# Expert rows scaled by their gates at eviction, and gathers that add into the result

## The reference, cut to what matters

```python
x = hidden_states                                   # 625 x 1024, after layernorm
capacity = ceil(2 * 1.25 * 625 / 8)                 # 196 slots for each of 8 experts
combine, dispatch = _top2_gating(x @ router_w, capacity)
expert_in = einsum('nec,nh->ech', dispatch, x)
hmid = silu(einsum('ech,ehf->ecf', expert_in, w1) + b1)
expert_out = einsum('ecf,efh->ech', hmid, w2) + b2
y = einsum('nec,ech->nh', combine, expert_out)      # two gates g1, g2 for each node
shared = silu(x @ sw1 + sb1) @ sw2 + sb2
out = y + 0.1 * shared
```

## Time and profile before

| | us |
|---|---|
| median of 3 runs | 1152.14 |
| lowest and highest | 1151.02, 1152.32 |
| the profiled execution, its own time | 1163.16 |
| its span | 1161.4 |
| busy in it: PE, PEld | 1099.8, 920.4 |
| busy in it: DVE, ACT, POOL | 697.3, 385.3, 380.6 |

### The profile page before, as it was taken

The page is one execution under the profiler, slowest core; times in us unless marked ns, Lnnn a source line. Parts: engine busy times, 40 slices in busy tenths (PEclk is TensorE's granted clock), DMA queues, the critical chain, the costliest instruction groups (busy, mean ns, idle before and its releaser), DMA issues.

```text
span 1161.4 us, 14333 instructions
## 1 busy us (share of the span) xinstructions
PE 1099.8 (95%) x5505; PEld 920.4 (79%) x5505; DVE 697.3 (60%) x1376; ACT 385.3 (33%) x599; POOL 380.6 (33%) x262
## 2 busy tenths in 40 slices
PE   5999999999999999994999999899979999999896
PEld 4878888888888888884999999887756878888774
DVE  8476666666655652100777676657378748866546
ACT  3222222222222222213223333362333415336652
POOL 6036556456556466651422132000020000310016
PEclk8999999999999999997999999899989999989997
DMA  8965677777666555539665543362242111588757
GB/s 326 416 199 131 157 198 203 204 205 178 160 159 151 120 119 118 112 49 268 186 205 165 176 120 100 103 208 91 73 76 88 30 62 38 218 260 262 246 179 247
DMA packets 84611, 191.77 MB, mean 165 GB/s; under 512 B 29079, under 2 KB 45274, under 8 KB 76088
## 3 DMA queue, kind: packets, MB, share of 16 engines
q1 hardware_dynamic: 36362, 123.40, 33.6%
q0 software_dynamic: 31968, 35.38, 14.4%
q10 hardware_dynamic: 16206, 32.00, 9.4%
HBM read 136.60 MB, written 54.15 MB: 164 GB/s over the span
## 4 chain that ended last, share of the span: by engine, by line
PE 72%; DMA 9%; DVE 8%; POOL 5%; issue 2%; ACT 2%; POOLq 0%; DVEq 0%; SPq 0%
PE ps L482 61%; POOL adj_scratch L1871 5%; DMA stage<-in_w_e 3%; DMA adj_scratch<-cnt,idx 3%; DVE rl L340 2%; PE ps L724 2%; PE ps L761 2%; PE ps L688 2%; DVE EQ L1248 1%; PE ps L472 1%; DMA stage<-h_scratch 1%; ACT rh L331 1%; PE ps L772 1%; DMA stage<-in_w_rel 1%; DMA AT<-adj_scratch 1%
## 5 line engine op out<-in xcount | busy, mean ns | idle before, releaser
L340 DVE TENSOR_TENSOR rl<-stage,rh 128x512 fp32r<-128x512 f32 (+1 forms) x288 | 228.7, 824 | 334.4 <-ACT rh L331 334.4
L331 ACT CAST rh<-stage 128x512 fp32r<-128x512 f32 (+1 forms) x288 | 193.7, 708 | 528.7 <-PE ps L482 289.7
L1871 POOL DMA_INDIRECT adj_scratch<-cnt,idx x162 | 261.5, 1614 | 224.3 <-DMA adj_scratch<-cnt,idx 81.5
L482 PE MATMUL ps<-rh,xTh 128*125 128x512 f32 x800 | 317.1, 396 | 2.0 <-DVE U L1316 1.7
L482 PE MATMUL ps<-rl,xTh 128*125 128x512 f32 x800 | 315.4, 394 | 0.0
L482 PE MATMUL ps<-rh,xTl 128*125 128x512 f32 x800 | 314.9, 394 | 0.0
L482 PE MATMUL ps<-rh,Ar 125*125 125x342 f32 x600 | 194.5, 329 | 20.6 <-DVE rl L340 10.9
L482 PE MATMUL ps<-rl,Ar 125*125 125x342 f32 x600 | 193.5, 327 | 0.0
L482 PEld LDWEIGHTS ps<-rh,xTh 128*125 128x125 f32 x800 | 148.7, 186 | 39.8 <-DVE U L1316 2.1
L482 PEld LDWEIGHTS ps<-rh,xTl 128*125 128x125 f32 x800 | 149.0, 186 | 37.3
L482 PEld LDWEIGHTS ps<-rl,xTh 128*125 128x125 f32 x800 | 149.0, 186 | 36.3
(11 more groups left out here) (263 smaller groups left out, 1195.5 us busy)
## 6 DMA issues: line engine op xcount, KB each, us to landing
stage<-in_w_rel SPq DMA_DIRECT2D x32, 1024.0 KB, 6.7
stage<-h_scratch SPq DMA_DIRECT2D x24, 855.0 KB, 6.5
stage<-in_w_e SPq DMA_DIRECT2D x16, 1024.0 KB, 6.1
adj_scratch<-Z POOLq DMA_DIRECT2D x16, 767.0 KB, 22.5
KR<-key_scratch ACTq DMA_DIRECT2D x27, 384.0 KB, 3.7
h_scratch<-He ACTq DMA_DIRECT2D x40, 257.0 KB, 10.1
h_scratch<-He ACTq DMA_DIRECT2D x40, 256.0 KB, 9.0
stage<-in_w_gate SPq DMA_DIRECT2D x8, 1024.0 KB, 6.3
```

Of the source, the lines that this page charges most:

```text
L331: e.copy(h, s).then_inc(*a_hi.up(*[("hi", t) for t in step(i)]))
L340: e.tensor_tensor(l, s, h.bitcast(F32), ALU.subtract).then_inc(*v_lo.up(*[("lo", t) for t in step(i)]))
L482: ins = e.matmul(ps[0:P, b, 0:width], a, m, start=first and n == 0, stop=last and n == len(parts) - 1)
L1871: e.indirect_dma_start(accd, bass.IndirectOffsetOnAxis(ap=idx[:, n:n + 1], axis=0), cnt[:, n:n + 1], None, compute_op=ALU.add).then_inc(*d ...
```

## The change

- A new array in memory, `gate_scratch`, one float for each slot, is zeroed by one more small store in the list of zeros. After the slots of expert 1 are asked for, POOL scatters g1 and g2 of every node to it (ten indirect transfers of 125 floats), waits for them, and loads it to `sg` (98 x 16, one column for each pair of expert and half; `sg[p, m]` is float 98 m + p). Slots of expert 2 and later are asked for behind that.
- ScalarE's copy to `EOs` becomes an ACTIVATE with a scale read from `sg`, and waits for `sg`.
- The ten gathers add into X, first all of k = 0, then all of k = 1, each in the order of chunks 3, 4, 0, 1, 2. They wait for X's second biases of their chunk, and the second for the first of the same chunk. The multiplications and additions of `combine`, ScalarE and POOL are gone.
- The second biases of half 1 for chunks 3 and 4 move from behind `routed_out(7)` to ahead of `routed_out(5)`, on TensorE and VectorE.
- `own`, VectorE's last additions and the stores go by halves first, then by chunks in the order 3, 4, 0, 1, 2, no longer by chunks and then halves. VectorE's last additions wait for both gathers of their chunk.

```diff
+    gated = nc.dram_tensor("gate_scratch", (128 * 23, 1), F32, kind="Internal").ap()
+        sg = sb("sg", [HC, 2 * 8], F32)
+        d_go, d_gi = count("gates_out", 16), count("gates_in", 16)
+        zeros.append((gated.rearrange("(p q) o -> p (q o)", p=128), Z[:, 0:23]))
-        gathered = [U128[:, i, :] for i in range(C)] + [G[:, i, :] for i in range(7, 10)] + [BA128[:], BB128[:]]
+        LAST = (3, 4, 0, 1, 2)
@@ sync
-            for c in range(C):
-                for hf in range(2):
+            for hf, c in [(hf, c) for hf in range(2) for c in LAST]:
@@ tensor
+                if n == 5:
+                    second_biases(1, range(3, C))
                 routed_out(n)
             routed_out(6)
             routed_in(7)
             second_biases(1, range(3))
             routed_out(7)
-            second_biases(1, range(3, C))
...
-                for j in range(2):
-                    on.wait_ge(*at("own low", j, hf))
+                on.wait_ge(*at("own low", 1, hf))
...
+            for hf in range(2):
+                for c in LAST:
+                    own(c, hf)
@@ scalar
-                        e.copy(EOs[:, m % 3, HALF[hf]], ps[0:HC, banks.of["out", n, j, hf], :]).then_inc(*a_out.up(("eo", n, j, hf)))
+                        on.wait_ge(*at("gates in"))
+                        e.activation(EOs[:, m % 3, HALF[hf]], ps[0:HC, banks.of["out", n, j, hf], :], ACT.Copy, scale=sg[:, m:m + 1]).then_inc(
+                            *a_out.up(("eo", n, j, hf)))
...
-            for c in range(1, C):
-                g = gathered[2 * c + 1]
-                on.wait_ge(*at("back", 2 * c + 1))
-                on.wait_ge(*at("comb"))
-                e.activation(g[0:P], g[0:P], ACT.Copy, scale=gs[:, 6, c:c + 1]).then_inc(*a_row.up(("back scaled", c)))
@@ vector
-            combine(0, 0)
-            combine(0, 1)
...
-            second_biases(1, range(3, C))
-            for c in range(C):
-                if c + 1 < C:
-                    combine(c + 1, 0)
-                for hf in range(2):
+            for hf, c in [(hf, c) for hf in range(2) for c in LAST]:
                     on.wait_ge(*at("own", c, hf))
-                    on.wait_ge(*at("y back", c, 1))
+                    on.wait_ge(*at("back", c, 1))
@@ pool
             for n in range(8):
                 slots_in(n)
-            for i, g in enumerate(gathered):
...
-                e.indirect_dma_start(g, None, eod, bass.IndirectOffsetOnAxis(ap=SI7[:, k, c:c + 1], axis=0)).then_inc(*d_g[i].up(("back", i)))
-            for c in range(1, C):
-                on.wait_ge(*at("back scaled", c))
-                on.wait_ge(*at("y back", c, 0))
-                e.tensor_tensor(X[:, c, :], X[:, c, :], gathered[2 * c + 1][0:P], ALU.add).then_inc(*p_row.up(("y back", c, 1)))
+                if n == 1:
+                    for c in range(C):
+                        for k in range(2):
+                            on.wait_ge(*at("SI"))
+                            on.wait_ge(*at("g12 scaled"))
+                            on.wait_ge(*at("slot zero"))
+                            e.indirect_dma_start(gated, bass.IndirectOffsetOnAxis(ap=SI[0:P, k, c:c + 1], axis=0), gs[:, 5 + k, c:c + 1], None).then_inc(
+                                *d_go.up(("gates out",)))
+                    on.wait_ge(*at("gates out"))
+                    e.dma_start(sg[:], gated[0:NS, :].rearrange("(m p) o -> p (m o)", p=HC), allow_slow_non_contiguous=True).then_inc(*d_gi.up(("gates in",)))
+            for k in range(2):
+                for c in LAST:
+                    for n, j in ((5, 1), (6, 0), (6, 1)):
+                        on.wait_ge(*at("eo out", n, j))
+                    for ev in (("SI7",), ("slot zero",), ("y b2", c, 0), ("y b2", c, 1)):
+                        on.wait_ge(*at(*ev))
+                    if k:
+                        on.wait_ge(*at("back", c, 0))
+                    e.indirect_dma_start(X[:, c, :], None, eod, bass.IndirectOffsetOnAxis(ap=SI7[0:P, k, c:c + 1], axis=0), compute_op=ALU.add).then_inc(
+                        *d_g[2 * c + k].up(("back", c, k)))
```

More of the change, by code:

```diff
@@ L856, in own @@
                 ins.then_inc(*product.up(("own", c, hf)))
-            own(0, 0)
-            own(1, 0)
-            own(0, 1)
-            for c in range(C):
-                if c:
-                    own(c, 1)
-                    if c + 1 < C:
-                        own(c + 1, 0)
-                banks.drop(("own", c, 0), ("own", c, 1))
+                banks.drop(("own", c, hf))
+            for hf in range(2):
+                for c in LAST:
+                    own(c, hf)
         def many_products(e, on, freed):
@@ L1712, in routed_out @@
                     lows(tile["e2", n, t // 2, t % 2] + RT)
-            def combine(c, k):
-                on.wait_ge(*at("back", 2 * c + k))
-                on.wait_ge(*at("comb"))
-                for hf in range(2):
-                    on.wait_ge(*at("y b2", c, hf))
-                if k:
-                    on.wait_ge(*at("y back", c, 0))
-                e.scalar_tensor_tensor(out=X[:, c, :], in0=gathered[2 * c + k][0:P], scalar=gs[:, 5 + k, c:c + 1], in1=X[:, c, :],
-                                       op0=ALU.mult, op1=ALU.add).then_inc(*v_row.up(("y back", c, k)))
             second_biases(0, range(C))
```

## The result

The changed kernel took 1182.37 us (median of 4 runs, 1174.39 to 1187.55) against 1151.58 (4 runs): 1.0268 times as long, with an interval of 1.0225 to 1.0311. The forecast, 1167, had the sign and half of the size, and the time lies above the range.

The account below looks back on a forecast made before the run. Weight loads, then TensorE, then gathers and the end relay bound the kernel. First gather 8.5 us later, gathers 11 longer, end 4.3 shorter: +15.2, scaled 15.1, giving 1167 us; range 1158 to 1177.

Parts of the forecast that it names:

- From T to L: First gather's start to last one's landing: 30.6 us, bounds 27.5 and 36.0, with DMA engines and not issue bounding.
- I take 25.5: Streaming of the ten adding gathers in us, chosen between 24.3 at 211 GB/s and 31 at the single adding load's 3.1.
- costs nothing: A chunk's second gather comes five gathers later, 12.8 us against 5.3 to land, so its wait adds 0.
- T, the gates' way: Gate scatters and sg load ahead of expert 2's slots make the first gather 3.5 us later, bounds 0 and 8.
- F: Start of the first row scatter, the common event of the traces; from it to the first gather 136.5 us was forecast.
- T, scaled evictions: ScalarE's 15 evictions on the chain, 0.1 us longer each: +1.5 us ahead of the first gather, bounds 0 and 2.
- T, biases: Second biases ahead of routed_out(5): 1.9 us of matmuls and 1.6 at lower clock, 3.5 taken, bounds 1.9 and 3.5.
- L to the end: Behind the last gather's landing: six VectorE operations in 4.0 us, last store issued 5.5 us behind it, 9.3 in all.
- The relay: Work behind the old gathers: scale, POOL add, VectorE, store; the change was to take away its 9.2 us.
- Issue: Rival: POOL's issue bounds the gathers, 21.9 us from first start to last landing; time 1158.6 us, chance 0.13.
- The elements: Rival: 4-byte packets alternate with weight-load packets, so every expert load slips; time above 1177 us, chance 0.04.
- Faster: Rival: gathers at plain price, 19.6 us; loop hides gates and evictions, matmuls' 1.9 stays; time 1149.8 us, chance 0.08.

Follow-up runs that it names:

- the kernel with the later wait: Kernel before plus gate scatters, sg load and scaled evictions, with POOL waiting for the scatters and loading sg only behind expert 3's slots: 1159.88 us, 1.0114.

## Why the prediction was wrong

**The step that failed** is the term for the stream in "From T to L", "I take 25.5": ten gathers priced at the rate of X<-in_fbias, as if that rate held whatever the row count. A gather of 125 rows is on five engines with 25 rows each. T to L was 47.9 us, not 30.6. The price of adding was read well: with 128 rows T to L is 31.9. The width, 16.0 us, was no term of the sum, and no rival had it. A sentence beside it failed too: that the second gather of a chunk waits for the first "costs nothing". With landings of 17.5 us and not 5.3 POOL waited for it 8.4 us in all, and the chain runs through it. The row that should have warned was X<-in_fbias: it is loaded in pieces of 112 and 13 rows, and 112 is seven times 16. I took its rate for a transfer of 125 rows in one piece, which isn't the same shape. The one row count in the diff that changed, from 128 to `[0:P]`, was read as nothing.

**T, the gates' way.** Forecast and measured, from F: slots of expert 2 asked for at 37.3 and 39.2 (the gate scatters hold POOL 1.18 us each, not 0.96), landed at 47.3 and 47.8. The second pair agrees by luck. The forecast had 3.5 us for 1,568 packets of single elements, and while sg was in flight (1028.8 to 1035 us) POOL's queue moved far fewer, slots' rows among them:

```profile
q0 software_dynamic: 224, 0.44, 39.9%
```

The slots themselves took 8.6 us from asking to landing, where the forecast had 6.5 and the 3.5 of packets. The first scaled eviction was forecast 3.5 us late and came 7.6 us late, at F + 55.7. Not all of it was still there at the first gather: 4.8 us in all with the biases' 1.9. Where the whole way ran by itself, it cost 11.0 us in the trace and 0.6%, 7 us, in time. F to T was forecast at 136.5, with bounds of 129.9 and 141.5; the six traces of this order have 132.5 to 145.6, 138.3 in the mean. So 3.5 was not wrong in kind, but one trace doesn't size it.

**T, scaled evictions.** 0.09 us more for each, as forecast. That 1.5 us of them add up on the chain isn't shown: the ratio, 0.9987, can't tell.

**T, biases.** 1.9 us of matmuls in both traces. The dip of the clock, 1.6 us, was 1.7 in the kernel with the biases alone and absent in both traces of the changed kernel.

**L to the end.** Forecast 9.3, measured 8.8, by its own steps: six VectorE operations in 4.04 us behind the last landing. SP's last issue in the changed kernel is here:

```profile
1176.42 0.81 SPq L462 DMA_DIRECT2D out<-X  x2
```

It comes 5.5 us behind L, as forecast. The relay did go, and its going gave 4.8 us, against which gathers that add cost 12.3 at full width.

**The sum.** Two small slips in it: the low bound of T to L is 27.9 by its own terms and not 27.5, the high one 36.1. Neither changes the range by more than 0.4 us.

**The rivals.** Issue did not bound the gathers (2.00 us each, 2.3 apart, where T to L is 4.8 for each). The elements did not hold the queue: sg landed 6.0 us behind its issue, and 14.2 in the kernel with the later wait. "Faster" needed T to L under 22.0; it was 31.9 even with 128 rows.

## What to carry to other kernels

Before pricing an indirect gather of rows, divide its row count: the largest divisor up to 16 is the number of engines that carry rows, so 125 rows have 5, 127 have 1 and 128 have 16. Where three spare rows can be afforded, gather 128. A gather that adds saves instructions on VectorE and POOL, but the ten took 1.6 times as long as plain ones (31.9 us against 19.6), so try it only where the DMA engines have the time; no run here shows such a place. And when a rate is taken from another transfer of the trace, compare the shapes first, not only the bytes.

## What the runs showed of the hardware

- An indirect gather of 4 KB rows by POOL puts 16 x (rows on an engine that has rows + 1) packets on the queue: 1,440, 1,600, 4,160 and 20,480 for ten gathers of 128, 126, 125 and 127 rows. The same 4 KB rows, one row less, take 148.9 us and not 31.9.
- 1,440 packets of 5.24 MB in all kept the 16 engines busy for 245 engine-us as plain gathers and for 441 as gathers that add.
- POOL's time to issue such a gather with adding grows with them: 1.54, 1.59, 2.00 and 4.70 us. Gate scatters of 125 numbers take 1.18 us, row scatters of 128 rows 0.96.
- The stretch at 1.2 GHz behind four float32 matmuls of depth 9 came in three traces (0.55, 0.57 and 0.60) and not in four.
- Ahead of the experts the traces differ by up to 26 us (the first row scatter starts between 978 and 1004 us), two traces of one kernel by 4 and 8 us, so differences were read from a common event, not from the span. Behind that event F to T still differs by 13 us between executions with the same instructions there.
